# A two-layer transformer stack on one core: row groups of both pairs issued together in a ring of six banks, one bank for a whole expert tile, and two small jobs moved between engines

## The chip, the core and the metric

The kernel runs on one core of a Trainium2 chip. The core has five engines, each with a queue of its own that is worked off in order: TensorE (PE: matmuls, with its weight loads shown apart as PEld), VectorE (DVE), ScalarE (ACT), GpSimd (POOL), and SyncE (SP), which here only starts DMAs. Engines are tied together by semaphores alone. The metric is the device time of one execution in microseconds (us). PSUM, into which TensorE writes, is used as eight banks of 128 x 512 fp32.

## What is computed

`x` is (4, 512, 128): four batches of 512 tokens. Two layers follow each other, each an attention and a mixture of experts, both behind a layer norm with scale and shift from `mod`:

```python
h = _layernorm(x) * (1 + ca) + sa
x = x + ga * _L0_attn_ref(h, ...)      # gated delta rule, 16 heads of 8
h = _layernorm(x) * (1 + cb) + sb
x = x + gb * _L0_ffn_ref(h, ...)       # 8 experts of 256, top 2, computed for every token
# the same again with _L1_attn_ref and _L1_ffn_ref

# first layer, attention, one step for each of the tokens of a scan:
S_new = at * S - at * bt * outer_Sk_k + bt * outer_v_k
ot = jnp.einsum('bhd,bhde->bhe', qt, S_new)

# second layer, attention: 16 heads, each with two 512 x 512 causal maps
A1 = jnp.einsum('bhqd,bhkd->bhqk', Q1, K1) * scaling
A2 = jnp.einsum('bhqd,bhkd->bhqk', Q2, K2) * scaling
attn = jax.nn.softmax(A1, -1) - lam * jax.nn.softmax(A2, -1)
O = jnp.einsum('bhqk,bhkd->bhqd', attn, V)      # then an RMS norm per head, and @ W_o.T

# second layer, 16 experts of 256, top 2, and a shared expert of 512
h = silu(xf @ W1[e] + b1[e]) * (xf @ W11[e] + b11[e])
y = y + (h @ W2[e] + b2[e]) * gates[:, e, None]
z = silu(xf @ Ws1 + bs1) * (xf @ Ws11 + bs11) @ Ws2 + bs2
```

## The kernel before

**Order.** The program is a list of small jobs, the same for all engines. A table gives each job a time (`table_layer0`, `table_layer1`), `LATE0` and `LATE` add for each engine and kind of job a shift, and each engine issues the jobs that it has a part in, sorted by the sum. The numbers only sort; what really starts when is left to the semaphores. In a table `t` and `e` are such times.

**First layer.** Four groups `g`. The tokens of a group are prepared (`conv`, `turned`, `tok_`, `k_t`, `vq_t`, ...: PE transposes, ACT and DVE copy), and solved in chunks of four tokens; then `scan` runs 32 steps, DVE L1143 to L1155 and ACT L1401 and L1412 in turn, each waiting for the other. Behind it `post_table` makes the output: `o_pw`, `o_dk` and `o_ol` are products inside a chunk, on POOL (L1580 to L1620), while PE sums over states. The experts follow (`moe0_table`): 16 units for each group, `up` on PE (L675 and L678, 512 columns each, into banks 0 to 2 in turn), silu on ACT (L1442), the product `hid` on DVE (L1179), `down` on PE (L700, bank 3), L1491 on ACT and L1632 on POOL. The experts of group g run beside the scan of group g + 1; those of the last group beside nothing but the start of the second layer. `tok_` (L1051) scales queries and keys by their length on DVE.

**Second layer, attention.** For each of four batches two halves of 12 `q` (`HALF` and `START` give them times). Heads are packed into row groups: the contraction over a head needs only few rows, so a matmul takes 32 of the array's 128 rows, and four maps lie at rows 0, 32, 64 and 96 of `QS` and `KS`. `top` (L738, and L741 adds the mask) makes scores for the row maximum, which DVE reduces (L1234); `top_t` (L753) turns the maxima. `score` (L765) makes the scores again, transposed, ACT takes the exponential (L1514), POOL clears what is not causal (L1668), and `weigh` (L779) multiplies by V. Both `top` and `score` handle the four row groups as two pairs: a job `pair` issues two matmuls side by side (rows 64*pair and 64*pair + 32) into two banks taken by `take_pair` from a ring of four (banks 0 to 3), then signals. `qk_in` (L719), `o_back` (L790) and `w_o` (L809) are what comes before and after.

**Second layer, experts.** `moe1_table(n)` for batch n: the shared expert in 4 units of 512 columns, then 23 tiles of 128 sorted token slots. For a tile, `up` makes both halves (L653 into bank 6, L658 into bank 4), ACT adds the bias (L1455) and takes a tanh (L1461), DVE makes `hid` (L1183, L1196), `down` (L688) writes a quarter of bank 5, and for every four tiles (`CHUNKS`) `keep` (L1474) copies bank 5 out. The weights of a tile, 386 KB, come by DMA into four buffers `wg` (`fetch`). Batches 0 to 2 run beside the attention halves of the next batches; batch 3 is what is left when attention is over, with the RMS norm, the norm, routing and the shared expert of batch 3 ahead of its tiles.

## Time and profile before

| | |
|---|---|
| median of 3 runs | 1538.91 us (1535.56 to 1539.24) |
| profiled execution | 1543.92 us, span 1542.2 us |
| PE busy in the span | 1138.1 us, 74% |
| DVE | 841.2 us, 55% |
| ACT | 608.2 us, 39% |
| POOL | 467.0 us, 30% |
| mean granted TensorE clock | 0.79 |

The span is that of the instructions; the profiled execution's own time holds 1.7 us more around it. A busy share is a mean over stages with different limits. By the trace's rows the first layer's scans run from 77 to 457 us; the second layer's first matmuls of `top` stand near 577 us, the first exponentials of its eight halves at 629.0, 712.6, 795.7, 907.0, 999.8, 1115.2, 1209.5 and 1308.7 us, and the last weighing ends at 1370.0 us. What is behind it belongs to the experts of the last two batches.

### The profile page before, as it was taken

Reading aid. Unit: us, or ns where it says so; the run is one execution under the profiler, and the core shown is the slowest. Engines: PE = TensorE matmul, PEld = TensorE weight load, DVE = VectorE, ACT = ScalarE, POOL = GpSimd, SP = SyncE. Lnnn points to the kernel's source line nnn. Section 1 sums busy time; section 2 is a strip of 40 time slices with the busy share of each in tenths; the row PEclk is TensorE's granted clock in tenths of the full one; section 3 lists DMA queues with packets and bytes.
Section 4 is the critical chain, followed back from the end, with each engine's and each line's share of the span. In section 5 each row is a group of like instructions: output and inputs, shape, how many; then the busy total and the mean of one; then the engine's idle time right before and its main releaser. Section 6 shows DMA issues by size and latency. Waiting matters only on the chain.

```text
span 1542.2 us, 17520 instructions
## 1 busy us (share of the span) xinstructions
PE 1138.1 (74%) x5780; PEld 645.5 (42%) x5780; DVE 841.2 (55%) x1927; ACT 608.2 (39%) x1353; POOL 467.0 (30%) x661
## 2 busy tenths in 40 slices
PE   6353446956768968888888888986888979885762
PEld 3131123433434533333334345653455644563551
DVE  1586888588862436544444546656556555244332
ACT  3343343543443431333243336543345623661241
POOL 0201624525437220112124131245221362344202
PEclk9675767978989986667566779988789967896696
DMA  6000000000000010000000023410123301350352
GB/s 194 1 0 1 0 1 0 1 1 1 1 0 0 1 62 0 1 1 1 0 1 0 1 75 94 118 44 21 50 65 114 98 26 49 110 166 26 118 161 71
DMA packets 53883, 64.65 MB, mean 42 GB/s; under 512 B 6544, under 2 KB 38304, under 8 KB 53792
## 3 DMA queue, kind: packets, MB, share of 16 engines
q1 hardware_dynamic: 51744, 59.33, 13.1%
q0 software_dynamic: 2048, 4.20, 0.9%
q8 instruction: 46, 0.75, 0.2%
q14 instruction: 45, 0.37, 0.1%
HBM read 52.83 MB, written 10.68 MB: 41 GB/s over the span
## 4 chain that ended last, share of the span: by engine, by line
PE 51%; DVE 22%; issue 9%; ACT 8%; POOL 6%; DMA 3%; SPq 0%; DVEq 0%; POOLq 0%; ACTq 0%
PE banks L779 6%; PE banks L719 6%; DVE MX L1234 4%; PE banks L738 4%; PE banks L700 3%; PE banks L675 3%; PE banks L678 3%; PE banks L765 3%; PE banks L520 3%; PE banks L741 3%; PE banks L653 2%; PE banks L658 2%; PE banks L688 2%; DMA wg<-in_ffn_dram 2%; PE banks L573 2%
## 5 line engine op out<-in xcount | busy, mean ns | idle before, releaser
L1234 DVE TENSOR_REDUCE MX<-banks 128x2 f32<-128x1024 f32 (+3 forms) x176 | 197.6, 1126 | 133.9 <-PE banks L741 129.6
L1514 ACT ACTIVATE PT<-banks 128x768 f32<-128x768 f32 (+1 forms) x192 | 168.4, 881 | 235.5 <-PE banks L765 230.2
L1668 POOL TENSOR_SCALAR_AFFINE_SELECT PT<-PT 128x256 f32<-128x256 f32 x256 | 102.2, 412 | 416.2 <-ACT PT L1514 415.8
L738 PE MATMUL banks<-KS,QS 32*128 32x512 f32 (+3 forms) x512 | 105.3, 460 | 48.1 <-DVE KS L1224 13.8
L700 PE MATMUL banks<-w,hid 128*128 128x128 f32 x512 | 79.7, 304 | 70.9 <-DVE hid L1179 70.9
L765 PE MATMUL banks<-QS,KS 32*128 32x256 f32 (+3 forms) x512 | 101.0, 441 | 25.7 <-DVE MX L1234 12.2
L1183 DVE SCALAR_TENSOR_TENSOR sil<-sil,yh 128x256 f32<-128x256 f32 (+1 forms) x108 | 50.2, 465 | 123.2 <-ACT sil L1461 122.3
L700 PEld LDWEIGHTS banks<-w,hid 128*128 128x128 f32 x512 | 70.1, 209 | 110.8 <-DVE hid L1179 98.1
L779 PE MATMUL banks<-PT,VA 128*17 128x512 f32 (+3 forms) x1024 | 110.7, 535 | 0.0
L738 PEld LDWEIGHTS banks<-KS,QS 32*128 32x128 f32 x512 | 50.8, 218 | 123.2 <-issue 39.5
L1179 DVE TENSOR_TENSOR hid<-banks,sil 128x512 f32<-128x512 f32 x64 | 43.9, 687 | 79.9 <-PE banks L678 75.6
L765 PEld LDWEIGHTS banks<-QS,KS 32*128 32x128 f32 x512 | 49.1, 214 | 89.1 <-issue 38.0
L1632 POOL TENSOR_TENSOR acc<-acc,yt 128x512 f32<-128x512 f32 x28 | 36.1, 1290 | 159.6 <-ACT yt L1491 159.6
L653 PE MATMUL banks<-xgT,wg 128*128 128x128 f32 x368 | 67.1, 309 | 23.5 <-DMA wg<-in_ffn_dram 18.3
L1412 ACT ACTIVATE T<-Sb,GM 128x32 f32<-128x32 f32 x128 | 44.6, 349 | 89.4 <-DVE Sb L1155 89.4
L1455 ACT ACTIVATE yh<-banks,wg 128x128 f32<-128x128 f32 x184 | 57.4, 365 | 52.1 <-PE banks L653 50.6
L675 PE MATMUL banks<-hTr,w 128*128 128x512 f32 x128 | 75.1, 673 | 0.0
L1442 ACT ACTIVATE sil<-banks 128x512 f32<-128x512 f32 x64 | 38.6, 604 | 85.1 <-PE banks L675 85.1
L658 PE MATMUL banks<-xgT,wg 128*128 128x128 f32 x368 | 64.0, 300 | 10.2 <-DVE hid L1196 9.9
L653 PEld LDWEIGHTS banks<-xgT,wg 128*128 128x128 f32 x368 | 53.4, 207 | 42.4 <-DMA wg<-in_ffn_dram 22.3
L678 PE MATMUL banks<-hTr,w 128*128 128x512 f32 x128 | 69.5, 626 | 0.0
L741 PE MATMUL banks<-maskb,identb 128*128 128x128 bf16 (+2 forms) x352 | 67.9, 283 | 0.0
(244 smaller groups left out, 2238.3 us busy)
## 6 DMA issues: line engine op xcount, KB each, us to landing
wg<-in_ffn_dram SPq DMA_DIRECT2D x92, 386.0 KB
xg<-xs SPq DMA_DIRECT2D x20, 256.0 KB, 2.9
yb<-ysb SPq DMA_DIRECT2D x20, 256.0 KB, 3.8
w<-in_ffn_w_dram SPq DMA_DIRECT2D x12, 256.0 KB, 5.9
xs<-zt SPq DMA_DIRECT2D x1, 1472.0 KB, 10.8
x<-in_L_attn_x_dram SPq DMA_DIRECT2D x4, 256.0 KB, 5.0
out_dram<-x SPq DMA_DIRECT2D x16, 64.0 KB, 1.5
wmod<-in_L_wmod_dram SPq DMA_DIRECT2D x2, 384.0 KB, 4.3
```

The lines of the kernel that those rows point to most:

```text
L653: mm = e.matmul(ps[:, 128 * fh:128 * fh + 128], w[:, 128 * fh:128 * fh + 128], h, start=True, stop=True)
L658: mm = e.matmul(ps[:, 128 * fh:128 * fh + 128], w[:, 256 + 128 * fh:384 + 128 * fh], h, start=True, stop=True)
L675: p_p1.at(e.matmul(ps[:, :], wa, h[:, :], start=True, stop=True))
L678: p_p3.at(e.matmul(ps[:, :], wb, h[:, :], start=True, stop=True))
L700: mm = e.matmul(ps[:, 128 * i:128 * i + 128], hid[u % 3][:, 128 * i:128 * i + 128], w2, start=(fh == 0 and i == 0), stop=end and not l, sk ...
L738: e.matmul(p4[:, k, m, :], QS[lo:lo + 32, (t0 + m) % 12, 128 * qb:128 * qb + 128], KS[lo:lo + 32, (t0 + m) % 12, 0:nk], start=(m == 0), st ...
L741: mm = e.matmul(p4[:, k, :, 128 * qb:128 * qb + 128], identb[:, :], maskb[:, :].unsqueeze(1).broadcast_to([128, nm, 128]), start=False, st ...
L765: mm = e.matmul(bank[i + k][:, c0:c0 + n], KS[lo:lo + 32, t % 12, 128 * kb:128 * kb + 128], QS[lo:lo + 32, t % 12, 128 * kb:512], start=Tr ...
L779: mm = e.matmul(o[32 * i4:32 * i4 + 17, 128 * kb:512], VAb[b % 2][:, kb, 2 * s + i4 // 2, :], PT[q % 3][:, i4, c0:c0 + n], start=(kb == 0) ...
L1234: v_mx.at(e.tensor_reduce(MX[n % 2][:, s0:s0 + nm, 2 * pair:2 * pair + 2, 24].rearrange("p s i -> p i s"), p4, AX.X, ALU.max, negate=True))
L1514: a_p.at(e.activation(PT[q % 3][:, 2 * pair:2 * pair + 2, :], where["score", q, pair][:, :, 0:n], ACT.Exp, scale=ISQ8))
L1668: ins = e.affine_select(out=pt, in_=pt, compare_op=ALU.is_ge, fill=0.0, base=0, pattern=[[0, 2], [1, 128]], channel_multiplier=-1)
```

## The change

The line numbers of the changed kernel differ by a few; `order` rows below carry its own.

1. `top` and `score` on PE issue both pairs in one job: four matmuls in turn over the four row groups, into two pairs of banks taken ahead. The job for pair 1 does nothing on PE; ACT and DVE still take pair by pair. In the tables pair 1 stands close behind pair 0.
2. The ring has six banks (0 to 5), and four while the shared expert adds up in bank 5. A tile of experts now has one bank for both `up` halves and the output of `down`: bank 6 for batches 0 to 2, one of the ring for batch 3. It is held until `keep` has copied the output, which now is done for each tile. ACT starts a tile when all four `up` matmuls are done (`p_p3`). The shared expert runs in 8 units of 256 columns.
3. `moe1_table` has tiles every 5.2, 5.2, 4.8 and 2.4 for the four batches (before: 3.9, 3.9, 3.9, 2.4), `down` 4.5 behind `up` (before 6), and DVE's `up` with a shift of 3.0 (before 4.0). `posi` exists twice.
4. In the first layer `tok_` goes from DVE (4 operations for a group) to ACT (8 activations with a scale for each group).
5. For the last group `o_pw`, `o_dk` and `o_ol` go from POOL to DVE, the table of what follows is drawn together, and its experts stand at +42 instead of +62. All units have `down` at +5 instead of +4, the steps are 4.6, 4.6, 4.0, 2.7 (before 4.6, 4.6, 4.6, 2.7), and DVE's `up` has a shift of 3.0 (before 2.5).
6. The second layer's `wq1`, `wk1`, `wv1` have memory that is free earlier, and are loaded once the last transposes of the preparation are done, ahead of the barrier between the layers.

```diff
-    DVE=dict(top=2.0, top_t=6.0, qk_in=2.0, up=4.0, down=1.0, route=2.0, place=0.0, w_o=2.0, rms=2.5),
...
+    DVE=dict(top=2.0, top_t=6.0, qk_in=2.0, up=3.0, down=1.0, route=2.0, place=0.0, w_o=2.0, rms=2.5),
...
-            for pair in range(2):
-                table.append((t, ("top", b, h, qb, s0, pair)))
-                t += step
+            table += [(t, ("top", b, h, qb, s0, 0)), (t + 1, ("top", b, h, qb, s0, 1))]
+            t += 2 * step
...
-        table += [(t, ("score", q, 0)), (t + step / 2, ("score", q, 1)), (t + 11, ("weigh", q))]
+        table += [(t, ("score", q, 0)), (t + 1.2, ("score", q, 1)), (t + 11, ("weigh", q))]
...
-    step = 3.9 if n < 3 else 2.4
+    step = (5.2, 5.2, 4.8, 2.4)[n]
...
-    for j in range(4):
-        table += [(e + 60 + 5 * j, ("up", 1, n, j)), (e + 72 + 4 * j, ("down", 1, n, j))]
+    for j in range(SHARED):
+        table += [(e + 60 + 2.6 * j, ("up", 1, n, j)), (e + 66 + 2.6 * j, ("down", 1, n, j))]
...
-            table += [(t, ("up", 1, n, 4 + j)), (t + 6, ("down", 1, n, 4 + j))]
+            table += [(t, ("up", 1, n, SHARED + j)), (t + 4.5, ("down", 1, n, SHARED + j)), (t + 5.7, ("keep", n, j))]
...
-        table.append((t + 7, ("keep", n, c)))
...
+        gq, state, pw, dk, ol, sums, out, step = 0, (1, 15), 5, 20, 21, (6, 20, 31), 34, 2.4
...
+        gq, state, pw, dk, ol, sums, out, step = 0, (1, 6), 1, 6.5, 7, (6, 12, 15), 17, 1.3
...
-        table += [(t + step * j, ("up", 0, n, j)), (t + step * j + 4, ("down", 0, n, j))]
+        table += [(t + step * j, ("up", 0, n, j)), (t + step * j + 5, ("down", 0, n, j))]
...
-        table += post_table(g, SCAN[g + 1]) + moe0_table(g, SCAN[g + 1] + 62, 4.6 if g < 3 else 2.7)
+        table += post_table(g, SCAN[g + 1]) + moe0_table(g, SCAN[g + 1] + (62 if g < 3 else 42), (4.6, 4.6, 4.0, 2.7)[g])
...
-                i = ring[0] % 4
-                ring[0] += 1
+                i = ring[0] % size[0]
+                ring[0] = i + 1
...
-                i = (ring[0] + 1) // 2 * 2 % 4
+                i = (ring[0] + 1) // 2 * 2 % size[0]
...
+                if l:
...
+                        parts = [(wg[t % 4][:, 128 * k:128 * k + 128], 128 * k, 128) for k in range(4)]
+                        h = xgT[(j - SHARED) // 4 % 2][:, 128 * (j % 4):128 * (j % 4) + 128]
+                    if n < 3:
+                        i, ps = 6, take(6)
+                        where["unit", u] = ps
+                    else:
+                        i, ps = take_ring(("unit", u))
+                    for w, at, cols in parts:
+                        mm = e.matmul(ps[:, at:at + cols], w, h, start=True, stop=True)
                     p_p3.at(mm)
-                    busy[4] = [(v_hid, u + 1)]
+                    busy[i] = [(v_hid, u + 1)] if j < SHARED else [(a_ys1, TILES * n + j - SHARED + 1)]
...
             def down(l, n, j):
...
+                if l and j >= SHARED:
+                    w = wg[(TILES * n + j - SHARED) % 4]
                     for fh in range(2):
-                        mm = e.matmul(ps[:, 128 * (j % 4):128 * (j % 4) + 128], hid[u % 3][:, 128 * fh:128 * fh + 128],
-                                      wg[t % 4][:, 512 + 128 * fh:640 + 128 * fh], start=(fh == 0), stop=(fh == 1),
-                                      skip_group_check=True)
+                        mm = e.matmul(where["unit", u][:, 0:128], hid[u % 3][:, 128 * fh:128 * fh + 128],
+                                      w[:, 512 + 128 * fh:640 + 128 * fh], start=(fh == 0), stop=(fh == 1))
                     p_y.at(mm)
-                    busy[5] = [(a_ys1, 6 * n + (j - 4) // 4 + 1)]
...
+                    if j == 0:
+                        size[0] = 4
+                        where["shared", n] = take(5)
...
+                        size[0] = 6
...
             def top(b, h, qb, s0, pair):
+                if pair:
+                    return
...
+                slots = [take_pair(("top", b, h, qb, s0, k)) for k in range(2)]
...
                 for m in range(nm):
-                    for k in range(2):
-                        lo = 64 * pair + 32 * k
-                        e.matmul(p4[:, k, m, :], QS[lo:lo + 32, (t0 + m) % 12, 128 * qb:128 * qb + 128],
-                                 KS[lo:lo + 32, (t0 + m) % 12, 0:nk], start=(m == 0), stop=False, skip_group_check=True)
-                for k in range(2):
-                    mm = e.matmul(p4[:, k, :, 128 * qb:128 * qb + 128], identb[:, :],
+                    for k in range(4):
+                        e.matmul(p4[k // 2][:, k % 2, m, :],
+                                 QS[32 * k:32 * k + 32, (t0 + m) % 12, 128 * qb:128 * qb + 128],
+                                 KS[32 * k:32 * k + 32, (t0 + m) % 12, 0:nk], start=(m == 0), stop=False,
+                                 skip_group_check=True)
+                for k in range(4):
+                    mm = e.matmul(p4[k // 2][:, k % 2, :, 128 * qb:128 * qb + 128], identb[:, :],
                                   maskb[:, :].unsqueeze(1).broadcast_to([128, nm, 128]), start=False, stop=True,
                                   skip_group_check=True)
-                p_mx.at(mm)
-                busy[i] = busy[i + 1] = [(v_mx, top_index(b, h, qb, s0, pair) + 1)]
+                    if k % 2:
+                        p_mx.at(mm)
+                for k, i in enumerate(slots):
+                    busy[i] = busy[i + 1] = [(v_mx, top_index(b, h, qb, s0, k) + 1)]
...
             def score(q, pair):
+                if pair:
+                    return
...
+                slots = [take_pair(("score", q, k)) for k in range(2)]
                 for kb, c0, n in STEPS[q % 3]:
-                    for k in range(2):
-                        lo = 64 * pair + 32 * k
-                        mm = e.matmul(bank[i + k][:, c0:c0 + n], KS[lo:lo + 32, t % 12, 128 * kb:128 * kb + 128],
-                                      QS[lo:lo + 32, t % 12, 128 * kb:512], start=True, stop=True,
+                    for k in range(4):
+                        mm = e.matmul(bank[slots[k // 2] + k % 2][:, c0:c0 + n],
+                                      KS[32 * k:32 * k + 32, t % 12, 128 * kb:128 * kb + 128],
+                                      QS[32 * k:32 * k + 32, t % 12, 128 * kb:512], start=True, stop=True,
                                       skip_group_check=True)
-                p_s.at(mm)
-                busy[i] = busy[i + 1] = [(a_p, 2 * q + pair + 1)]
+                        if (kb, c0, n) == STEPS[q % 3][-1] and k % 2:
+                            p_s.at(mm)
+                for k, i in enumerate(slots):
+                    busy[i] = busy[i + 1] = [(a_p, 2 * q + k + 1)]
...
-                    if w == 0:
-                        src = src[:, :, :, 4 * f:4 * f + 4]
-                    v_tok.at(e.tensor_tensor(
-                        tok[w][:, :, f, :].rearrange("p r (b h) -> p b h r", b=4), src,
-                        sn[:, 4 * w:4 * w + 4].unsqueeze(2).unsqueeze(3).broadcast_to([128, 4, 16, n]), ALU.mult))
...
+            def o_pw(g, i):
+                if g < 3:
+                    return
+                n, o = 4 - i, (0, 4, 7, 9)[i]
+                Q4 = Qb[g % 2][:, :, :].rearrange("p (c j) r -> p c j r", j=4)
+                W4 = Wb[g % 2][:, :, :, :]
+                v.wait_ge(a_vq, 2 * g + 2)
...
+                m = v_own.at(e.tensor_tensor(PW[:, :, 0:n, :], Q4[:, :, i:4, :],
...
+            def tok_(g, w):
...
+                a.wait_ge(p_kt if w else p_vq, 2 * g)
...
+                    if w:
+                        s4 = src[:, b, :, :].rearrange("p h e -> p e h").unsqueeze(2).broadcast_to([128, 8, 2, 16])
+                    else:
+                        s4 = src[:, b, :, :].rearrange("p h (f r) -> p r f h", f=2)
+                    ins = e.activation(tok[w][:, :, :, 16 * b:16 * b + 16], s4, ACT.Copy, scale=sn[:, 4 * w + b:4 * w + b + 1])
+                a_tok.at(ins)
...
+            def keep(n, j):
+                c = j // 4
+                u = 64 + UNITS[1] * n + SHARED + j
+                a.wait_ge(p_y, u + 1)
+                a.wait_ge(d_ys[c % 2], 16 * (3 * n + c // 2))
+                a_ys1.at(e.activation(ysb[c % 2][:, j % 4, :], where["unit", u][:, 0:128], ACT.Copy, scale=0.5))
...
             def o_pw(g, i):
+                if g == 3:
+                    return
...
-            sp.wait_ge(s_layer0, 4)
+            for used, n in ((p_cv, 12), (p_kt, 8), (p_vq, 8)):
+                sp.wait_ge(used, n)
             load(wq1[:, :], "wq1", d_qk1)
             load(wk1[:, :], "wk1", d_qk1)
             load(wv1[:, :], "wv1", d_vo1)
+            sp.wait_ge(s_layer0, 4)
```

Below, PE's order in the second layer's attention, at one place of half 1, before the change. A row is a matmul with what it reads and the size of it, and how often it follows itself.

```order
L765 MATMUL banks<-QS,KS 128x512 x2
L719 MATMUL banks<-hTr,wk 128x512
L738 MATMUL banks<-KS,QS 128x384 x2
L741 MATMUL banks<-maskb,identb 128x128 x2
L753 MATMUL banks<-ident,MX 128x128 x4
L765 MATMUL banks<-QS,KS 128x512 x2
L738 MATMUL banks<-KS,QS 128x384 x2
L741 MATMUL banks<-maskb,identb 128x128 x2
```

And the same place in the changed kernel (L778 is its `score`, L746 and L751 its `top`, L795 its `weigh`).

```order
L778 MATMUL banks<-QS,KS 128x512 x4
L726 MATMUL banks<-hTr,wk 128x512
L746 MATMUL banks<-KS,QS 128x384 x4
L751 MATMUL banks<-maskb,identb 128x128 x4
L765 MATMUL banks<-ident,MX 128x128 x4
L795 MATMUL banks<-PT,VA 17x256 x4
L795 MATMUL banks<-PT,VA 17x128 x4
L778 MATMUL banks<-QS,KS 128x384 x4
```

What stood as two blocks of two, with other work between them, stands as one block of four.

PE's order where the first layer's experts begin, before the change: L675 and L678 are one unit's `up`, L700 its `down`.

```order
L675 MATMUL banks<-hTr0,w1_0 128x512
L678 MATMUL banks<-hTr0,w3_0 128x512
L700 MATMUL banks<-w2_0,hid0 128x128 x4
L675 MATMUL banks<-hTr0,w1_0 128x512
```

And in the changed kernel (L677 and L680 `up`, L716 `down`).

```order
L677 MATMUL banks<-hTr0,w1_0 128x512
L680 MATMUL banks<-hTr0,w3_0 128x512
L677 MATMUL banks<-hTr0,w1_0 128x512
L680 MATMUL banks<-hTr0,w3_0 128x512
L716 MATMUL banks<-w2_0,hid0 128x128 x4
L677 MATMUL banks<-hTr0,w1_0 128x512
```

The `up` of the next unit now stands between a unit's `up` and its `down`.

PE's order behind the last weighing (the last row of L779), where tiles of batch 2 are still open, before the change: L653 and L658 are a tile's `up`, L688 is `down`, by `hid` of three tiles in turn.

```order
L779 MATMUL banks<-PT2,VA1 17x128 x4
L688 MATMUL banks<-wg3,hid0 128x128 x2
L653 MATMUL banks<-xgT1,wg1 128x128 x2
L658 MATMUL banks<-xgT1,wg1 128x128 x2
L790 MATMUL banks<-ident,OV 128x128 x4
L639 MATMUL banks<-ident,xg0 128x128 x4
L688 MATMUL banks<-wg0,hid1 128x128 x2
```

And in the changed kernel, further on: L689 is `down`, L667 all four matmuls of an `up`, L643 turns a chunk's tokens, L483 turns `xn` of batch 3.

```order
L689 MATMUL banks<-wg0,hid2 128x128 x2
L667 MATMUL banks<-xgT0,wg1 128x128 x4
L643 MATMUL banks<-ident,xg1 128x128 x3
L689 MATMUL banks<-wg1,hid0 128x128 x2
L667 MATMUL banks<-xgT1,wg2 128x128 x4
L483 MATMUL banks<-ident,xn1 128x128 x4
L689 MATMUL banks<-wg2,hid1 128x128 x2
L667 MATMUL banks<-xgT1,wg3 128x128 x4
```

Before, `down` of a tile stood behind `up` of the next; now each `down` stands directly ahead of the next tile's `up`. Between the last weighing and the transposes of `xn` there were 10 `down` and 9 `up`, and none behind; now there are 9 of each, and three more tiles of batch 2 end behind those transposes.

## Rows read from the trace of the kernel before

**Rows 1.** The page, its first lines: span and busy time

```profile
span 1542.2 us, 17520 instructions
...
PE 1138.1 (74%) x5780; PEld 645.5 (42%) x5780; DVE 841.2 (55%) x1927; ACT 608.2 (39%) x1353; POOL 467.0 (30%) x661
```

**Rows 2.** Stretches: us, busy (x count), granted clock, DMA share, GB/s

```profile
257.00:369.00 112.00, 78.95 (x294) 44.88 (x294) 85.85 (x219) 48.06 (x150) 49.12 (x54) 0.85 0.00 1
369.00:457.00 88.00, 63.67 (x240) 34.95 (x240) 67.70 (x179) 36.16 (x122) 41.49 (x46) 0.90 0.00 1
457.00:511.00 54.00, 47.28 (x192) 25.34 (x193) 14.83 (x36) 18.72 (x45) 36.75 (x40) 0.97 0.00 1
511.00:552.40 41.40, 40.40 (x183) 25.03 (x183) 13.37 (x27) 16.94 (x45) 9.93 (x12) 0.99 0.00 1
577.00:629.00 52.00, 43.59 (x152) 17.56 (x152) 35.36 (x46) 6.90 (x11) 0.72 (x1) 0.59 0.00 0
629.00:795.70 166.70, 141.57 (x688) 57.73 (x688) 73.04 (x103) 58.68 (x79) 28.85 (x73) 0.66 0.00 1
795.70:1308.70 513.00, 436.29 (x2659) 249.78 (x2660) 290.72 (x569) 226.73 (x399) 167.11 (x264) 0.83 0.19 57
1308.70:1365.20 56.50, 50.11 (x388) 33.18 (x388) 16.89 (x51) 38.71 (x74) 17.97 (x39) 0.91 0.39 120
1445.00:1517.00 72.00, 48.71 (x295) 43.06 (x295) 23.80 (x69) 30.03 (x80) 0.00 (x0) 0.87 0.49 137
```

**Rows 3.** The page's groups: busy us, mean ns, idle before

```profile
L1234 DVE TENSOR_REDUCE MX<-banks 128x2 f32<-128x1024 f32 (+3 forms) x176 | 197.6, 1126 | 133.9 <-PE banks L741 129.6
...
L738 PE MATMUL banks<-KS,QS 32*128 32x512 f32 (+3 forms) x512 | 105.3, 460 | 48.1 <-DVE KS L1224 13.8
...
L765 PE MATMUL banks<-QS,KS 32*128 32x256 f32 (+3 forms) x512 | 101.0, 441 | 25.7 <-DVE MX L1234 12.2
...
L653 PE MATMUL banks<-xgT,wg 128*128 128x128 f32 x368 | 67.1, 309 | 23.5 <-DMA wg<-in_ffn_dram 18.3
```

**Rows 4.** Timeline of PE in half 1: start, us in which all ran

```profile
699.36 0.79 PE L738 MATMUL banks<-KS,QS 32*128 32x512 f32 x2
...
700.90 0.79 PE L765 MATMUL banks<-QS,KS 32*128 32x512 f32 x2 [0.42 <-DVE QS L1224]
```

**Rows 5.** DVE's waits from 257 to 457 us: us, count, longest

```profile
DVE Sb L1155 <- ACT T L1412: 23.2, 17, 4.0
DVE hid L1179 <- PE banks L678: 13.0, 7, 3.6
```

**Rows 6.** Groups: `tok_` in 257 to 369 us; L1491 in 457 to 514 us

```profile
L1051 DVE TENSOR_TENSOR tok<-banks,sn 128x512 f32<-128x512 f32 (+1 forms) x4 | 2.9, 814 | 0.0
...
L1491 ACT ACTIVATE yt<-banks,gatew 128x128 f32<-128x128 f32 x24 | 6.9, 372 | 12.2 <-PE banks L700 12.2
```

**Rows 7.** Timelines behind the last scan: POOL's products, and DVE

```profile
457.30 1.10 POOL L1580 TENSOR_TENSOR GQ<-Q,GM 128x512 f32<-128x512 f32 x1
...
488.08 0.72 POOL L1620 TENSOR_TENSOR OL<-OL,OTm 128x256 f32<-128x256 f32 x1
...
460.44 0.69 DVE L1179 TENSOR_TENSOR hid<-banks,sil 128x512 f32<-128x512 f32 x1 [3.03 <-PE banks L678]
```

**Rows 8.** Timelines of one tile of batch 2 behind attention

```profile
1379.89 0.61 PE L653 MATMUL banks<-xgT,wg 128*128 128x128 f32 x4
...
1380.49 0.71 PE L658 MATMUL banks<-xgT,wg 128*128 128x128 f32 x4
...
1380.53 0.63 ACT L1455 ACTIVATE yh<-banks,wg 128x128 f32<-128x128 f32 x2 [1.20 <-PE banks L653]
...
1382.16 0.61 DVE L1196 SCALAR_TENSOR_TENSOR hid<-banks,wg,sil 128x128 f32<-128x128 f32 x2
```

**Rows 9.** Timeline of PE: last weighing, then `xn` of batch 3

```profile
1369.18 0.84 PE L779 MATMUL banks<-PT,VA 128*17 128x256 f32 x16
...
1403.15 1.25 PE L479 MATMUL banks<-ident,xn 128*128 128x128 f32 x4 [3.06 <-DVE xn L904]
```

More of the change, by code:

```diff
@@ L340, in build @@
         posf = sb("posf", [128, 2, 4])
[L341 removed]
+        posi = [sb(f"posi{i}", [128, 2, 4], mybir.dt.uint32) for i in range(2)]
         gt_ = sb("gt_", [128, TILES, 16])
@@ L691, in down @@
                     p_y.at(mm)
-                    busy[5] = [(a_ys1, 6 * n + (j - 4) // 4 + 1)]
                     return
-                ex, fh = (j // 2, j % 2) if l == 0 else (0, j)
-                end = fh == (3 if l else 1)
-                iy = 5 if l else 3
-                ps = take(iy) if fh == 0 else bank[iy]
-                w2 = ws2[:, fh, :] if l else w2_0[:, ex, fh, :]
-                for i in range(4):
-                    mm = e.matmul(ps[:, 128 * i:128 * i + 128], hid[u % 3][:, 128 * i:128 * i + 128], w2,
-                                  start=(fh == 0 and i == 0), stop=end and not l, skip_group_check=True)
@@ L708, in down @@
+                ex, fh = j // 2, j % 2
+                ps = take(3) if fh == 0 else bank[3]
+                for i in range(4):
+                    mm = e.matmul(ps[:, 128 * i:128 * i + 128], hid[u % 3][:, 128 * i:128 * i + 128], w2_0[:, ex, fh, :],
+                                  start=(fh == 0 and i == 0), stop=(fh == 1), skip_group_check=True)
                 p_y.at(mm)
-                if l == 0:
-                    busy[iy] = [(a_yt, 8 * n + ex + 1)]
-                else:
-                    busy[iy] = [(v_acc, 5 * n + 1)]
+                busy[3] = [(a_yt, 8 * n + ex + 1)]
```

263 lines of the change are left out of this document (142 added, 121 removed).

## The prediction

> **What bounds the kernel now.** I read the page first: PE is busy for 74% of the span and no other engine for more than 55% [rows 1]. That is a mean, so I cut the span into stretches by what runs there and read each engine's busy time and the granted clock [rows 2]. Three kinds come out.
>
> In the scans (257 to 457 us) DVE leads: 85.9 of 112 and 67.7 of 88 us. The scan is a ping-pong with ACT, so DVE's gaps lengthen it: it waits 23.2 us for ACT's T and 13.0 us for the experts' `up` [rows 5].
>
> Behind the last scan (457 to 552 us) PE is busy for 47.3 of 54 and then 40.4 of 41.4 us [rows 2]. The last group's experts fill it.
>
> In the eight attention halves, 629 to 1365 us and nearly half the span, PE is busy 141.6 of 166.7, 436.3 of 513.0 and 50.1 of 56.5 us: 628 of 736, or 85%. DVE and ACT stand at 381 and 324 us. What is taken off PE there shortens the time until another engine's chain is late. Behind the halves come tiles in series, at 72 us for the last 23 of them with PE at 48.7, a chain of hand-offs [rows 2, 8].
>
> **Merged row groups.** In the page's groups `top` (L738) has 512 records of 460 ns, 235.5 us in all, but 105.3 us busy; `score` (L765) 512 of 441 ns, 225.8, but 101.0 [rows 3]. So the two row groups of a pair already run side by side, and the timeline shows it: two matmuls of 512 columns in 0.79 us [rows 4]. If four do what two do, 105.3 + 101.0 = 206.3 us becomes 103. An eighth of `top`, 13.2 us, belongs to the first half's and lies ahead of 629; its saving of 6.6 stands beside DVE's reductions (35.4 us busy of 52 there), I take **-6**. The rest, 103 - 6.6, is on the engine that bounds the halves: **-96**. The mask matmuls (L741), `weigh` and the projections are as many as before. Bounds: 0 (the array runs no more than two at once, or the pace passes to another engine) and -103 for both together.
>
> The trace has no group of four. The Trainium skill, "TensorE: Matmul & The Clock Gate", Part 3 on packing small matmuls, gives four row groups a measured speed-up of 3.07 over one after another, not 4. Against two side by side that would save 1 - 2/3.07 = 35% of 206.3, some 72 us, and by it the sum would be 30 us higher, 1467; this trace's pairs gain the full factor of 2, so I stay with a half.
>
> **One bank for a tile.** Before, the next tile's first half could be written as soon as ACT had read bank 6. Now `up`, silu, `hid`, `down` and `keep` of a tile all end before the next `up`. From the timeline of a tile: `up` 0.61 + 0.71 = 1.3 us on PE, from ACT's start to the end of `hid` 1382.77 - 1380.53 = 2.2 us, and ACT starts later than now, behind the whole `up` [rows 8]. With `down` of 0.6 and a `keep` of 128 x 128 like L1491, 0.37 us [rows 6], the loop is 4.5, with its hand-offs about 4.6 us; with PE's 1.9 us stretched where its clock stands at 1.2 GHz, rather 5.8. The table puts a tile at 5.2 or 4.8 of its units and a half at 80; with halves of some 84 us that is 5.4 and 5.0 us. So the loop fits at the higher clock and not at the lower. The 69 tiles of batches 0 to 2 could stall PE by nothing or by 5.8 - 4.6 = 1.2 each (83 us); I take a third, 0.4: **+28**. `keep` by tile, the shared expert's smaller pieces and the doubled `posi` are hidden by ACT's 56% and DVE's 48% idle in the halves; uncovered, 51 extra copies of 0.37 would cost 19 us, which is inside the 83.
>
> **The scans.** With `up` of the next unit ahead of `down`, PE has `up` ready when DVE comes, and `up` comes later on DVE: this goes for the 13.0 us. `tok_` takes 2.9 us a group off DVE and puts eight activations of 0.37, 3.0 us, on ACT [rows 6], in a ping-pong that needs both: net nothing for three groups beside scans, at worst 9 us either way, since the first of the four is prepared ahead of any scan. Of the 37 us of waits I take half: **-19**, bounds 0 and -38.
>
> **Behind the last scan.** POOL's products run from 457.3 to 488.8 us, 31.5 us; DVE meanwhile is busy 14.8 of 54 us [rows 7, 2]. On DVE the chain takes perhaps 12 us, and 20 would go. But PE has 6.7 and 1.0 us of idle time from 457 to 552, and its work does not shrink, though a longer overlap with the second layer's start may take in a little: **-9**, bounds 0 and -10. DVE has `hid` to make there too (0.69 us at 460.44, after 3 us of waiting); covered. The early loads of `wq1` save a transfer that nothing waits for in any shown row: 0.
>
> **Tiles behind attention.** Before, from the last weighing (ending 1370.0) to the transposes of `xn` PE took 33 us with 10 `down` and 9 `up` [rows 9]. PE issues in order, so the norm's path waits for each tile ahead of it. Nine loops now take 9 x 5.2 = 47: +14, and three tiles behind the transposes lie before routing is over: +4. **+18**, bounds 8 (loops of 4.6) and 28 (of 5.8 and full cost of the three). The last 23 tiles now use a ring of six banks, so that loop binds nobody, but each `down` stands ahead of the next `up`, which frees its weight buffer a tile sooner: 3.13 us a tile now, of which the page shows 18.3 us of waits for `wg` in all [rows 3]. With three tiles in flight in a loop of 6.3, a tile could take 2.1, the same as PE's 48.7/23. I take 2.35: **-18**, bounds 0 and -23.
>
> **Sum.** -96 - 6 + 28 - 19 - 9 + 18 - 18 = -102. The profiled execution has 1543.9 us (span 1542.2 and 1.7 around it), which gives 1442; it lies 5.0 us over the median, so **1437** against 1538.9.
>
> **Rivals.** A difference under 0.3%, 4.6 us, could not be told from none.
>
> *The forecast's mechanism, 1400 to 1475*, 0.62: PE's saving comes through, with stalls between none and twice those taken.
>
> *The pace passes to the evictions, 1475 to 1520*, 0.17. A merged `top` needs four banks of six, and gives them back only after two reductions, 2 x 1.13 = 2.25 us [rows 3]; 88 of them less 11 ahead of 629 are 77. With 0.6 uncovered in each it is +46: 1483. With the tile loop fully exposed (+55 over the sum) it is 1492; both together 1538. For it speaks that DVE already waits at every `top` for PE and now gets two at once; against it, 381 and 324 us of 736. The Trainium skill, "TensorEngine Tiling (Array Packing)", Performance Considerations, warns that packing speeds up TensorE but not the emptying of PSUM, which may become the bottleneck; no row of before shows it.
>
> *Slower, by the clock*, 0.07. The granted clock is 0.66 from 629 to 795.7, where only attention runs, and 0.83 and 0.91 in the halves with experts (means over both levels, 1.2 and 2.4 GHz) [rows 2]. If stalls between merged blocks bring it down in those six halves as well, their PE work of 486 - 72 = 414, with masks about 420 us, grows by 420 x (0.84/c - 1). It decides from 0.68 down, where this is the whole 102; at 0.66 it is +115: 1552. Against it: 577 to 629, PE with gaps, is low, but the halves keep nearly as much PE work in less time.
>
> *No gain from merging*, 0.05: the four run as two pairs, and -102 is 0. Then 1539, with the rest of the sum cancelling. The pairs' overlap speaks against.
>
> *Better, 1388*, 0.09: no stalls of the tile loop (-28), and in the first two halves, with denser PE work, the clock rises from 0.66 to 0.83: (141.6 - 38) x (1 - 0.66/0.83) = 21.
>
> **Chances.** Faster: 0.62 + 0.09, nearly all of 0.17, a little of 0.05: 0.89. The same 0.04. Slower 0.07. Range: from the better case to the upper part of the second, 1385 to 1515; outside lie the slower case, the no-gain case and edges, 0.18. The forecast's own is 1400 to 1475.
>
> **What would show it.** In the changed kernel's groups `top` and `score` should have about 103 us busy in place of 206 for the same 1024 records, four starting together with 0.79 us. PE's waits for ACT's `keep` should stay under 40 us in the halves, DVE's wait for L678's successor in the scans near nothing, and its wait for T no longer than 23. POOL's last product of group 3 moves to DVE and `xn` follows some 20 us sooner, with PE full behind it. From the last weighing to the transposes of `xn` I expect some 47 us, and 2.35 us a tile at the end. I am wrong if the two groups stay above 150 us, if DVE's reductions or ACT's exponentials are what PE waits for in most blocks, or if the halves' clock falls under 0.75.

## The result and the profile after

The change made the kernel slower: 1568.2 us (median of 4) against 1537.2 of before, measured together; ratio 1.0189 [1.0151, 1.0227]. 1437 with a range to 1515 was forecast.

The page of the changed kernel, first lines and the groups that answer to [rows 3] (L746 is its `top`, L778 its `score`, L1276 its row maximum, L667 all its expert `up` matmuls of the second layer; the last figures are the idle time ahead, and who ended it):

```profile
span 1566.8 us, 17963 instructions
...
PE 1073.9 (69%) x5844; PEld 651.8 (42%) x5844; DVE 847.8 (54%) x1963; ACT 625.8 (40%) x1485; POOL 454.6 (29%) x641
...
L1276 DVE TENSOR_REDUCE MX<-banks 128x2 f32<-128x1024 f32 (+3 forms) x176 | 192.3, 1123 | 88.6 <-PE banks L751 88.4
...
L667 PE MATMUL banks<-xgT,wg 128*128 128x128 f32 x736 | 131.6, 335 | 36.8 <-ACT ysb L1530 30.7
...
L778 PE MATMUL banks<-QS,KS 32*128 32x256 f32 (+3 forms) x512 | 52.7, 441 | 64.0 <-DVE MX L1276 57.5
...
L746 PE MATMUL banks<-KS,QS 32*128 32x512 f32 (+3 forms) x512 | 53.0, 457 | 59.9 <-ACT PT L1569 39.9
```

`top` and `score` are busy for 52.7 + 53.0 = 105.7 us, where they were 206.3 [rows 3]: the merging does all that was expected of it. But ahead of these two groups PE now idles 123.9 us instead of 73.8, and the names have changed: `score` waits for the row maximum 57.5 us (12.2 before), `top` for the exponentials 39.9. PE's busy time fell by 64 us and the span grew by 25.

Two views of the halves. Stretches of the changed kernel: halves 1 and 2, then 4 to 8 (columns as in [rows 2]).

```profile
607.80:744.80 137.00, 103.10 (x692) 45.55 (x696) 71.40 (x103) 56.12 (x80) 29.06 (x72) 0.76 0.00 1
...
848.50:1379.90 531.40, 391.13 (x2583) 252.66 (x2584) 249.64 (x522) 228.23 (x459) 147.65 (x248) 0.79 0.21 62
```

The kernel before in its halves 4 to 8:

```profile
907.00:1365.20 458.20, 393.20 (x2598) 236.88 (x2596) 250.94 (x512) 225.66 (x412) 149.85 (x252) 0.87 0.25 74
```

PE is busy for the same 391 and 393 us there. Multiplied by the granted clock it is 309 and 342 us of work at 2.4 GHz, so 33 us were saved; at the old clock the 309 would be 355. The lower clock (0.79 instead of 0.87) gives 36 us back, and PE's idle time goes from 65.0 to 140.3. These are estimates, since the mean clock of a stretch counts PE's idle time too: record by record, each at the clock granted to it, the work is 295 and 339 us, 44 saved and 49 given back. PE's waits over all eight halves of the changed kernel, by who ended them (us, times, longest):

```profile
PE banks L778 <- DVE MX L1276: 57.0, 35, 3.7
PE banks L746 <- ACT PT L1569: 39.9, 29, 2.6
PE banks L689 <- DVE hid L1239: 25.7, 23, 1.9
PE banks L667 <- ACT ysb L1530: 24.8, 45, 1.4
```

The upper two are the banks of merged blocks, the lower two the tile's loop through one bank. How the first comes about shows in half 1, PE and then DVE by start and duration:

```profile
642.21 0.45 PE L746 MATMUL banks<-KS,QS 32*128 32x384 f32 x4 [0.24 <-ACT PT L1569]
642.59 0.40 PE L751 MATMUL banks<-maskb,identb 128*128 128x128 bf16 x4
642.91 0.84 PE L795 MATMUL banks<-PT,VA 128*17 128x384 f32 x8
644.49 0.51 PE L778 MATMUL banks<-QS,KS 32*128 32x512 f32 x4 [0.74 <-DVE MX L1276]
...
642.73 0.75 DVE L1266 SCALAR_TENSOR_TENSOR KS<-HR,selk,banks 128x512 fp32r<-128x512 f32 x1 [1.94 <-ACT HR L1555]
643.39 1.82 DVE L1276 TENSOR_REDUCE MX<-banks 128x2 f32<-128x768 f32 x2
```

A `top` of all four row groups is made in 0.78 us with its mask, and takes DVE 1.82 us to empty. The next `score` wants four banks, two of which the first of the two reductions (0.91 us each) must give back, and starts 0.2 us after its end, with PE idle for 0.74. That the two engines take turns shows in the page: the row maxima wait 88.4 us for PE, and `score` 57.5 us for the row maxima. (The 1.94 us of DVE above are a wait for ACT's `HR`.)

Four abreast take 0.51 us for 512 columns. That is at a granted clock of 1.00, and the 0.79 us of two abreast [rows 4] was at 0.50. At equal clock four take what two take: two of before at 1.00, then four of the changed kernel at 0.50.

```profile
655.10 0.50 PE L765 MATMUL banks<-QS,KS 32*128 32x512 f32 x2 [0.21 <-DVE MX L1234]
...
652.89 0.80 PE L746 MATMUL banks<-KS,QS 32*128 32x512 f32 x4 [0.57 <-ACT PT L1569]
```

### The profile page after: what moved, and what is told of

Same layout as the page of the kernel before. It is cut to its first block, busy times and chain, and to the rows that moved or that the text cites. A ratio compares the mean times of both kernels' runs of the same rounds, so it can differ in the third digit from the quotient of the medians.

```text
span 1566.8 us, 17963 instructions
## 1 busy us (share of the span) xinstructions
PE 1073.9 (69%) x5844; PEld 651.8 (42%) x5844; DVE 847.8 (54%) x1963; ACT 625.8 (40%) x1485; POOL 454.6 (29%) x641
## 4 chain that ended last, share of the span: by engine, by line
PE 44%; DVE 19%; ACT 13%; issue 13%; POOL 8%; DMA 2%; SPq 0%; ACTq 0%; POOLq 0%; DVEq 0%
PE banks L667 8%; DVE MX L1276 6%; PE banks L726 4%; PE banks L795 3%; PE banks L689 3%; ACT PT L1569 3%; PE banks L524 3%; PE banks L746 2%; ACT yh L1510 2%; PE banks L716 2%; POOL QX L1644 2%; DVE hid L1239 2%; DVE sil L1226 2%; PE banks L751 2%; PE banks L778 2%
## 5 line engine op out<-in xcount | busy, mean ns | idle before, releaser
L1276 DVE TENSOR_REDUCE MX<-banks 128x2 f32<-128x1024 f32 (+3 forms) x176 | 192.3, 1123 | 88.6 <-PE banks L751 88.4
L1569 ACT ACTIVATE PT<-banks 128x768 f32<-128x768 f32 (+1 forms) x192 | 162.6, 877 | 154.3 <-PE banks L778 154.0
L1226 DVE SCALAR_TENSOR_TENSOR sil<-sil,yh 128x256 f32<-128x256 f32 x124 | 53.1, 428 | 235.8 <-ACT sil L1516 235.4
L667 PE MATMUL banks<-xgT,wg 128*128 128x128 f32 x736 | 131.6, 335 | 36.8 <-ACT ysb L1530 30.7
L667 PEld LDWEIGHTS banks<-xgT,wg 128*128 128x128 f32 x736 | 114.5, 238 | 55.2 <-issue 50.8
L689 PE MATMUL banks<-wg,hid 128*128 128x128 f32 x368 | 75.7, 338 | 55.2 <-DVE hid L1239 55.1
L795 PE MATMUL banks<-PT,VA 128*17 128x512 f32 (+3 forms) x1024 | 109.8, 534 | 0.0
L716 PEld LDWEIGHTS banks<-w,hid 128*128 128x128 f32 x512 | 70.0, 204 | 75.9 <-DVE hid L1222 56.6
L716 PE MATMUL banks<-w,hid 128*128 128x128 f32 x512 | 74.6, 292 | 35.9 <-DVE hid L1222 29.3
L778 PE MATMUL banks<-QS,KS 32*128 32x256 f32 (+3 forms) x512 | 52.7, 441 | 64.0 <-DVE MX L1276 57.5
L689 PEld LDWEIGHTS banks<-wg,hid 128*128 128x128 f32 x368 | 60.0, 230 | 82.3 <-DVE hid L1239 74.8
L746 PE MATMUL banks<-KS,QS 32*128 32x512 f32 (+3 forms) x512 | 53.0, 457 | 59.9 <-ACT PT L1569 39.9
L1693 POOL TENSOR_TENSOR acc<-acc,yt 128x512 f32<-128x512 f32 x28 | 36.7, 1312 | 160.9 <-ACT yt L1546 160.8
L680 PE MATMUL banks<-hTr,w 128*128 128x512 f32 x128 | 72.5, 651 | 15.2 <-ACT sil L1497 15.2
L677 PE MATMUL banks<-hTr,w 128*128 128x512 f32 x128 | 74.6, 668 | 0.0
L746 PEld LDWEIGHTS banks<-KS,QS 32*128 32x128 f32 x512 | 26.6, 217 | 107.1 <-ACT PT L1569 42.7
L778 PEld LDWEIGHTS banks<-QS,KS 32*128 32x128 f32 x512 | 26.4, 209 | 103.0 <-issue 54.5
L577 PE MATMUL banks<-QX,sumh 128*64 128x512 f32 x64 | 38.0, 749 | 44.6 <-POOL QX L1644 44.5
```

Source lines behind the costliest of these rows:

```text
L667: mm = e.matmul(ps[:, at:at + cols], w, h, start=True, stop=True)
L677: p_p1.at(e.matmul(ps[:, :], wa, h[:, :], start=True, stop=True))
L689: mm = e.matmul(where["unit", u][:, 0:128], hid[u % 3][:, 128 * fh:128 * fh + 128], w[:, 512 + 128 * fh:640 + 128 * fh], start=(fh == 0), ...
L716: mm = e.matmul(ps[:, 128 * i:128 * i + 128], hid[u % 3][:, 128 * i:128 * i + 128], w2_0[:, ex, fh, :], start=(fh == 0 and i == 0), stop=( ...
L746: e.matmul(p4[k // 2][:, k % 2, m, :], QS[32 * k:32 * k + 32, (t0 + m) % 12, 128 * qb:128 * qb + 128], KS[32 * k:32 * k + 32, (t0 + m) % 1 ...
L778: mm = e.matmul(bank[slots[k // 2] + k % 2][:, c0:c0 + n], KS[32 * k:32 * k + 32, t % 12, 128 * kb:128 * kb + 128], QS[32 * k:32 * k + 32, ...
```

## The experiments

All ratios are against the kernel before, run on the same chip. The stages come from each profiled execution: the start of the second layer's first exponential, then the halves by the starts of their exponentials (the last by the end), then what is behind. Each row adds up to its span. Spans are to be compared with care where chips differ: the median of the kernel before was 1548.5 us beside l0only, merge4, unmerged and twobanks, 1539.2 beside sixfirst, close, downring and halfreduce, and 1540.9 beside the rest.

| run | ratio | to the first exponential | halves 1, 2 | half 3 | halves 4 to 8 | behind | span |
|---|---|---|---|---|---|---|---|
| before | 1 | 629.0 | 166.7 | 111.3 | 458.2 | 177.0 | 1542.2 |
| changed | 1.019 | 607.8 | 137.0 | 103.7 | 531.4 | 186.9 | 1566.8 |
| l0only | 0.990 | 613.2 | 167.2 | 103.6 | 469.2 | 175.8 | 1529.0 |
| merge4 | 1.090 | 649.6 | 199.6 | 123.7 | 534.6 | 182.2 | 1689.7 |
| unmerged | 0.960 | 602.0 | 118.7 | 97.8 | 468.0 | 188.0 | 1474.5 |
| twobanks | 1.025 | 604.4 | 135.5 | 94.3 | 576.2 | 174.6 | 1585.0 |
| sixfirst | 0.941 | 600.5 | 119.1 | 90.2 | 455.5 | 176.6 | 1441.9 |
| close | 0.982 | 600.7 | 123.1 | 101.5 | 505.7 | 182.8 | 1513.8 |
| downring | 0.946 | 601.7 | 118.8 | 97.7 | 456.6 | 169.3 | 1444.1 |
| halfreduce | 0.981 | 602.3 | 116.4 | 100.2 | 501.1 | 186.4 | 1506.4 |
| sixtail | 0.935 | 600.5 | 118.4 | 91.7 | 455.4 | 171.7 | 1437.7 |

For unmerged and downring the profiled execution was 8 to 10 us under the median; their ratios, not their spans, say how they stand.

**Which part.** The first four runs took the change apart. The edits are hunks of the diff above.

l0only: the diff's first-layer parts (4, 5, 6) on the kernel before.

> The kernel before with the changes of the first layer alone (tables, queries and keys on ScalarE, last group's products on VectorE, early loads). In the profile of the changed kernel the first exponential of the second layer comes 21 us sooner (607.8 instead of 629.0). Theory A, the first layer's parts give this and nothing behind them takes it back: 1516 us. Rival, the second layer gives it back, by its clock or its DMAs: 1530 to 1540.

0.990 [0.987, 0.993]. The first layer's parts are worth 1%, between the two theories (1516 us is 0.985 of before, 1530 is 0.994). The first exponential comes 15.8 us sooner, not 21.

merge4: `top` and `score` of the diff on the kernel before, and in its tables

```diff
-            for pair in range(2):
-                table.append((t, ("top", b, h, qb, s0, pair)))
-                t += step
+            table += [(t, ("top", b, h, qb, s0, 0)), (t + 0.01, ("top", b, h, qb, s0, 1))]
+            t += 2 * step
-        table += [(t, ("score", q, 0)), (t + step / 2, ("score", q, 1)), (t + 11, ("weigh", q))]
+        table += [(t, ("score", q, 0)), (t + 0.01, ("score", q, 1)), (t + 11, ("weigh", q))]
```

> The kernel before with merged top and score alone, in the old ring of four and with the old tiles; pair 1 stands right behind pair 0 in the tables. Theory A, the one bank for a tile is what eats the gain: merging alone pays, 1440 to 1480. Theory B, evictions eat it: a block holds all four banks, so that the next can't start before two reductions of 1.12 us or two exponentials of 0.88 us are done; 88 blocks of the one kind and 96 of the other make 366 us of eviction in series: slower than before, 1560 to 1620.

1.0902 [1.0874, 1.0931], 1689 us: theory B, and beyond its range. Even the first exponential comes 20.6 us later, with the first layer untouched. PE's two longest waits in the halves:

```profile
PE banks L738 <- ACT PT L1522: 56.2, 34, 2.1
PE banks L770 <- DVE MX L1242: 53.0, 29, 4.4
```

unmerged: the changed kernel with `top` and `score` on PE and their table entries as before.

```diff
-                slots = [take_pair(("score", q, k)) for k in range(2)]
+                i = take_pair(("score", q, pair))
-        table += [(t, ("score", q, 0)), (t + 1.2, ("score", q, 1)), (t + 11, ("weigh", q))]
+        table += [(t, ("score", q, 0)), (t + step / 2, ("score", q, 1)), (t + 11, ("weigh", q))]
```

> The changed kernel with top and score in two jobs of a pair again, each at its old place; ring of six, one-bank tiles and the new tables stay. Theory A, one bank for a tile costs what was gained: no better than the changed kernel, 1565 to 1600, since the merging's saving is lost as well. Theory B, evictions of four banks at once cost it: near 1516 to 1530, the kernel before with the first layer's gain.

0.9600 [0.9576, 0.9624], better than either theory. Against it, the changed kernel with its merging is 6% slower, while it halves the work of the matmuls that it touches. It costs in seven of the eight halves, the first two included, which have no tiles beside them; only the last is shorter merged (65.8 against 72.4 us). The reason is in their stretch:

```profile
602.00:720.70 118.70, 109.76 (x692) 47.37 (x690) 71.49 (x103) 58.43 (x79) 28.39 (x72) 0.84 0.00 1
```

Its PE work is 109.8 x 0.84 = 92 us at full clock, that of before 141.6 x 0.66 = 93 [rows 2]: the same. The ring of six took 16 us of idle time out (25.1 to 8.9) and the clock rose from 0.66 to 0.84, worth 32 us more. Merged it is 103.1 x 0.76 = 78, 14 us less work, but 33.9 us idle.

twobanks: the changed kernel with tiles in two banks, and the ring down to four from the first unit of the shared expert. Its tables also put pair 1 only 0.01 behind pair 0, as merge4's do.

```diff
                     if n < 3:
-                        i, ps = 6, take(6)
+                        size[0] = 4
+                        i = (6, 4)[j % 2]
+                        ps = take(i)
...
-                        size[0] = 6
+                        size[0] = 6 if n == 3 else 4
```

> The changed kernel with tiles of batches 0 to 2 in banks 6 and 4 in turn and a ring of four from the first tile on, pair 1 right behind pair 0 in the tables. Theory A: PE's 20 us of waits for keep and 18.5 us for hid between 848 and 1314 us go, and with them part of the lower clock: 1490 to 1520. Theory B: four banks instead of six for merged blocks make the waits for the reductions (36.7 us there) and exponentials (18.3) several times longer: 1590 to 1640.

1.0252 [1.022, 1.0284]: theory B's direction, at 1587 a little under its range. The waits for `keep` are gone from the head of the list; PE waits longer for the exponentials instead, and idles 182 us in halves 4 to 8, where the changed kernel idles 140. There `score` waits 31.0 us for the row maximum (36.7 in the changed kernel), `top` 25.9 for the exponentials (18.3), and L728, the projections, 14.4:

```profile
PE banks L780 <- DVE MX L1278: 31.0, 12, 3.7
PE banks L748 <- ACT PT L1571: 25.9, 14, 3.1
PE banks L691 <- DVE hid L1241: 21.8, 16, 2.5
PE banks L728 <- ACT PT L1571: 14.4, 12, 1.5
```

**What in the merging costs, and what in unmerged gains.** Four runs more.

sixfirst: l0only with `size = [6]` in the ring, and at the head of PE's `up`

```diff
+                if l:
+                    size[0] = 4
```

> The kernel before with the first layer's changes and a ring of six banks until the first matmul of the shared expert, of four from then on; nothing merged, old tiles, old tables of the second layer. Theory, the ring's size and not the row work set the pace of the halves: the first two halves (83.9 and 83.3 us in the run with the first layer alone) come down to the 61.1 and 57.6 of the run with pairs unmerged, their granted clock from 0.67 to 0.84, and 35 to 50 us of 1529 go: 1480 to 1495, ratio 0.96 to 0.97. Rival, that run's gain was in its tables and its one-bank tiles: halves stay over 78 us.

0.9411 [0.937, 0.9452], 1446 us: the theory, and more than it gave. The ring of six alone, in use until the first matmul of the shared expert at 778 us, takes 48 us from halves 1 and 2 and 13 from half 3, and 13 ahead of them. The 14 us less in halves 4 to 8, where the ring is four again, are within what identical kernels scatter there.

```profile
600.50:719.60 119.10, 110.34 (x694) 47.70 (x690) 71.81 (x103) 58.45 (x80) 28.86 (x73) 0.83 0.00 1
```

close: unmerged with the merged version's table entries.

```diff
-        table += [(t, ("score", q, 0)), (t + step / 2, ("score", q, 1)), (t + 11, ("weigh", q))]
+        table += [(t, ("score", q, 0)), (t + 1.2, ("score", q, 1)), (t + 11, ("weigh", q))]
```

> The changed kernel with two matmuls to a job again, but the tables of the merged version: pair 1 stands 1.0 or 1.2 behind pair 0, with what falls between them still between. Tells whether merging loses by taking four banks at once and signalling late, or by bunching the two pairs in the order. Theory, the four banks in one grip: close to the run with pairs unmerged (0.96, first halves 58 to 62 us). Rival, the bunching: close to the changed kernel (1.02, first halves 68 us).

0.9824 [0.9786, 0.9861]: between the two. Bunching the pairs costs 2.2 of the 6 points, nearly all of it where tiles run too (505.7 against 468.0 us); taking and giving four banks in one grip costs the other 3.7, by the profiles 14 us in halves 1 and 2, 2 in half 3 and 26 in halves 4 to 8. The last half alone is shorter merged (65.8 against 75.5 us).

halfreduce: the changed kernel with a shorter row maximum, which leaves out the second half of the keys.

```diff
-                                        p4, AX.X, ALU.max, negate=True))
+                                        p4[:, :, :, 0:nk // 2], AX.X, ALU.max, negate=True))
```

> The changed kernel with the row maximum taken over the first half of the keys alone (the other half is left out), which cuts the mean of its 176 reductions from 1.12 to some 0.65 us and changes nothing else. Theory, PE waits in merged blocks until the reductions give back the banks: PE's 48 us of waits for MX fall below 20, the clock rises, ratio 0.97 to 0.99 instead of 1.02. Rival, the reductions only cover other waits (exponentials, tiles): 1.01 to 1.02.

0.9809 [0.9777, 0.984]: inside the theory's range, and outside the rival's.

```profile
L1276 DVE TENSOR_REDUCE MX<-banks 128x2 f32<-128x512 f32 (+3 forms) x176 | 107.1, 637 | 86.7 <-PE banks L751 86.7
```

DVE has 85 us less to do, on an engine that was busy for 54% of the span, and 60 us of the span go; halves 1 and 2 come down from 137.0 to 116.4. Its detail was off: PE's waits for MX fell from 57.0 to 34.4 us, not below 20. It shows that the row maxima are on the path of the changed kernel. That merging put them there it does not show alone: the same cut in unmerged was not run. What speaks for it is that in unmerged's halves `score` waits 2.5 us for MX and `top` 7.3.

downring: unmerged with `down` of batches 0 to 2 in a ring bank.

```diff
+                    if n < 3:
+                        i, where["y", u] = take_ring(("y", u))
+                        busy[i] = [(a_ys1, TILES * n + j - SHARED + 1)]
-                        mm = e.matmul(where["unit", u][:, 0:128], ...
+                        mm = e.matmul(where["y", u][:, 0:128], ...
```

> The run with pairs unmerged, but the output of down for batches 0 to 2 goes to a bank of the ring, so that the tile's bank 6 is free once hid is made and not only after keep. Theory, the tile's loop through one bank is what is left on PE's path there: PE's 21.5 us of waits for keep in 818 to 1286 us go, the waits for hid stay, ratio 0.94 to 0.95. Rival, the ring's banks are dearer than the wait: 0.96 to 0.98.

0.9455 [0.9421, 0.9489], as the theory said: holding the tile's bank until `keep` costs 1.5%. By the profiled executions it is 11 us in halves 4 to 8, which is within their scatter, and 19 behind them, which is not.

**The first layer, and a better kernel.** For the parts of the first layer the runs are near the limit of what their intervals part.

moe0new: before with `down` at +5, the new steps and DVE's shift of 3.0 alone.

```diff
-        table += [(t + step * j, ("up", 0, n, j)), (t + step * j + 4, ("down", 0, n, j))]
+        table += [(t + step * j, ("up", 0, n, j)), (t + step * j + 5, ("down", 0, n, j))]
```

> The kernel before with the order and steps of the first layer's experts alone (down at +5, steps 4.6, 4.6, 4.0, 2.7, VectorE's up with a shift of 3.0). Theory, this is what shortened the scans: VectorE's 13.0 us of waits for PE behind hid fall to about 3 as in the run with the first layer's changes, the last scan ends some 10 to 19 us sooner, ratio 0.988 to 0.995. Rival, the move of queries and keys did it: scans as before, ratio 0.998 to 1.002.

0.9908 [0.9881, 0.9936]. The last scan ends at 441.0 instead of 456.6 us. DVE's waits from 257 to 441 us (compare [rows 5]):

```profile
DVE Sb L1155 <- ACT T L1412: 17.6, 14, 2.5
DVE hid L1179 <- PE banks L678: 2.8, 3, 1.9
```

tokdve: l0only with `tok_` on DVE.

```diff
+            def tok_(g, w):
+                v.wait_ge(v_own, pr["sn"])
...
-            def tok_(g, w):
-                a.wait_ge(v_sn, g + 1)
```

> The kernel before with the first layer's changes except that queries and keys are scaled on VectorE as before. The run with all of the first layer had 0.990. Theory, the move nets to nothing, since ScalarE's eight activations take as long as VectorE's four operations and the scan needs both: 0.988 to 0.994. Rival, VectorE alone bounds the scans and 2.9 us a group come back: 8 us slower, 0.995.

0.9930 [0.9902, 0.9958], which overlaps l0only's interval. Scans end at 441.4, with `tok_` on ACT at 438.0: if the move is worth something, it is about 3 us.

g3pool: l0only with the last group's products on POOL, in their old table, and its experts at +62.

```diff
-        table += post_table(g, SCAN[g + 1]) + moe0_table(g, SCAN[g + 1] + (62 if g < 3 else 42), (4.6, 4.6, 4.0, 2.7)[g])
+        table += post_table(g, SCAN[g + 1]) + moe0_table(g, SCAN[g + 1] + 62, (4.6, 4.6, 4.0, 2.7)[g])
```

> The kernel before with the first layer's changes except that the last group's local products stay on GpSimd, with their old table, and its experts at +62. Theory, PE's work fills the stretch behind the last scan anyway, and the move is worth little: 0.990 to 0.994. Rival, GpSimd's 31 us chain was on the path to the second layer: 9 us and more slower, 0.996 to 1.0.

0.9862 [0.9826, 0.9898]: not slower than l0only, and under the range that the theory gave. From the last scan to the first exponential it takes 177.1 us, l0only 175.2. PE's longest wait of that stretch in this run, and then in l0only:

```profile
PE banks L479 <- DVE xn L904: 14.4, 2, 10.0
```

```profile
PE banks L483 <- DVE xn L908: 10.1, 2, 10.0
```

One wait of 10.0 us for a norm stands in both; the move took off the other 4, and the stretch is 2 us shorter.

sixtail: sixfirst with the last batch's tiles in ring banks.

```diff
+                    if n == 3:
+                        i3, ps = take_ring(("unit", u))
+                        p3 = ps[:, 256:512]
...
-                    ps = take(5) if j % 4 == 0 else bank[5]
+                    iy = (5, 6)[(j - 4) // 4 % 2] if n == 3 else 5
+                    ps = take(iy) if j % 4 == 0 else bank[iy]
```

> The run with six banks at first (0.941) with the last batch's tiles in ring banks: both halves of up in one bank of the ring of four, held until hid is made, and down's output in banks 5 and 6 by chunks. Theory, the tail is a loop of two tiles through banks 6 and 4; with four tiles' room the last stretch shortens by 5 to 12 us: 0.933 to 0.938. Rival, the weights' DMA or PE's own work bounds that stretch: 0.941.

0.9345 [0.9315, 0.9376], 1440 us: the best here, inside the theory's range, and 4.9 us shorter behind the halves by the profile, a little under the 5 to 12 that it gave. Its interval touches sixfirst's, so that the gain on it is not beyond doubt.

## Why the prediction was wrong

By the ratios: the first layer's parts gave 1.0 points, the ring of six 4.9, the one-bank tiles with their tables took 1.9, and the merging 5.9. The sum is the 1.9 measured, and must be: each step is one run against the run before it in this order. In another order a part weighs otherwise, as the merging does with 9.0 points on a ring of four.

**The step that failed** is "The rest, 103 - 6.6, is on the engine that bounds the halves: -96". The work did go; the time did not follow. I read 85% busy as a bound. But a pair's banks come back one eviction at a time, and with four banks PE's work and DVE's or ACT's could hardly overlap across blocks. Merging makes the piece of work between two evictions shorter and the number of banks it needs twice as large. Merge4 and unmerged show that merging loses, with four banks (+9.0 points) and with six (+5.9). That the evictions are why rests on PE's waits, 57.0 us for row maxima and 39.9 for exponentials at the merged blocks, and on halfreduce (-3.8 points for a shorter maximum), which has no counterpart on unmerged; for the exponentials no run was made, nor for `top` or `score` merged alone. Close shares the loss out. My rival had the mechanism, and priced it at 0.6 us a block for `top` alone, +46. The changed kernel against unmerged is a loss of 92 us by the spans (91 by the ratios), where the two terms of the merging had -102. The Trainium skill, "TensorEngine Tiling (Array Packing)", Performance Considerations, which I had cited beside that rival, agrees with those runs.

Of the signs that I had named, the good ones came: 105.7 us for the two groups, 24.8 us of waits for `keep`, 2.6 us of DVE's waits behind `hid` and 22.3 for T in the scans. The bad one did not come as worded: in the halves PE waits for a reduction 35 times beside 96 merged `score` blocks, and for an exponential 29 times beside at most 88 `top` blocks, which is about a third of them and not most.

**A term that was missing** is the ring of six by itself. I counted it only as what merged blocks need; sixfirst measures it at 4.9 points, 75 us. (The spans give 1529.0 - 1441.9 = 87, on two chips of which one is 9 us slower with the same kernel.) The rows had it: PE's busy time in halves 1 and 2 was at a clock of 0.66, so its 85% was no floor, and much of the gain is the clock's.

**The slower rival**, by the clock alone, had the right sign. The clock in halves 4 to 8 fell to 0.79, above the 0.75 at which I had said I would be wrong. It cost some 36 to 49 us there (the two estimates above) beside 75 of idle time, where this mechanism alone was to cost 102.

**Terms that held.** The scans: -19 forecast, 456.6 to 437.3 measured, of which the order of the experts gives 15.6; it was PE's lateness behind `hid`, as said. To the transposes of `xn` 47 us were expected behind the last weighing: they start at 1436.18, 48.3 us after it. The last tiles: 2.35 us expected, 2.42 measured (22 steps between the first matmuls of the 23 tiles, at 1484.3 and 1537.6 us). These rows, last weighing and `xn`, answer to [rows 9]:

```profile
1387.06 0.84 PE L795 MATMUL banks<-PT,VA 128*17 128x256 f32 x16
...
1436.18 1.06 PE L483 MATMUL banks<-ident,xn 128*128 128x128 f32 x4
```

**Terms mis-sized.** The tile's single bank: +28 was for the halves, and 0 net behind them. Unmerged against sixfirst is 1.9 points, 29 us, in all. By the profiles 11.4 of them lie behind the halves; the 7.6 in half 3 and 12.5 in 4 to 8 are within the scatter there, so that the +28 is neither borne out nor refuted. The last group's products: -9 forecast, 177.1 to 175.2 measured between scan and first exponential, -2, and no gain in the ratio. The first `top`s: -6 forecast, but the changed kernel's first exponential comes 5.8 us after unmerged's, and PE waits 13.3 us for row maxima at L746 ahead of it; merging costs there as well. Besides PE's work, which I had reckoned as the floor, one wait of 10.0 us for `xn` stands there whoever makes the products; what holds it was not tried. Two figures of the working had no row: the 37 us of waits in the scans are 36.2 [rows 5], and for the 38 us that the better case takes off PE in halves 1 and 2 the trace has 28.4, half of the two groups' 56.8 there. Neither moves the forecast.

**Open.** Why the clock stands where it does: in halves 1 and 2 PE idles 15% at 0.66 (before), 25% at 0.76 (changed), 7.5% at 0.84 (unmerged) and 24% at 0.87 (halfreduce), so the idle share alone does not order it. And five kernels with the same jobs in the second layer (before, l0only, moe0new, tokdve, g3pool) have 104 to 111 us in half 3 and 451 to 469 us in halves 4 to 8, so that differences of less than some 8 and 18 us there say nothing from single profiles.

## What to carry over

Before taking work off a busy engine, ask how its buffers come back: here a block that is produced faster than it is emptied, in a grip of four banks, bought waiting. Add buffers first and measure that alone; here two banks more were worth 5%, and what they were meant to make possible cost 6%. The 85% at a clock of 0.66 was not a floor: multiply busy time by the granted clock before calling an engine the bound.

## What the hardware showed that I had not expected

Four row groups side by side cost no more than two: 512 records of 457 and 441 ns in 53.0 and 52.7 us busy, where pairs had 105.3 and 101.0 [rows 3]: four take 51% of the time of two and two. The Trainium skill's 3.07 ("TensorE: Matmul & The Clock Gate", Part 3) is against one after another, which no record here shows; with a full factor of 2 for pairs it would have left 65%, and the measured 51% decides. And the clock moved more time than the idle gaps did: in halves 1 and 2 two banks more removed 16 us of idle time and, by the clock, 32 us of busy time with the same work.
